# Two row maxima over the mask bytes, moved to later steps of the attention loop

## The reference

```python
scores = einsum('bsd,bmd->bsm', layernorm(x), ctx) * scale
scores = where(memory_mask[:, None, :], scores, -1e30)
readout = einsum('bsm,bmd->bsd', softmax(scores), ctx)
valid_b = any(memory_mask, axis=-1)          # one flag per sequence
x = x + where(valid_b[:, None, None], readout, 0)
```

## Time and profile before

| | before |
|---|---|
| median of 3 runs | 218.23 us (218.16 to 218.25) |
| the profiled execution, time | 218.16 us |
| the profiled execution, span in the trace | 216.4 us |
| PE busy | 209.1 us, 97% |
| DVE busy | 162.7 us, 75% |
| ACT busy | 131.1 us, 61% |
| POOL busy | 93.9 us, 43% |

### The profile page before, as it was taken

The page is one execution under the profiler, slowest core; times in us unless marked ns, Lnnn a source line. Parts: engine busy times, 40 slices in busy tenths (PEclk is TensorE's granted clock), DMA queues, the critical chain, the costliest instruction groups (busy, mean ns, idle before and its releaser), DMA issues.

```text
span 216.4 us, 4415 instructions
## 1 busy us (share of the span) xinstructions
PE 209.1 (97%) x1392; PEld 174.0 (80%) x1392; DVE 162.7 (75%) x448; ACT 131.1 (61%) x248; POOL 93.9 (43%) x83
## 2 busy tenths in 40 slices
PE   7899999998998999999999999999999999999995
PEld 2687677775686899889889899899898898898893
DVE  3789699778668658888898777686785785786754
ACT  3549898768522614766866676675765666676340
POOL 7799999305002010247535733623614615516000
PEclk9999999999999999999999999999999999999999
DMA  5995430000000000022452144043042142110002
GB/s 166 331 386 183 145 101 2 3 2 3 0 0 0 3 2 0 0 75 75 145 148 79 67 145 145 1 145 128 17 145 92 53 145 64 82 48 0 0 0 98
DMA packets 8062, 17.45 MB, mean 81 GB/s; under 512 B 960, under 2 KB 3184, under 8 KB 7920
## 3 DMA queue, kind: packets, MB, share of 16 engines
q1 hardware_dynamic: 7616, 16.97, 23.9%
q10 hardware_dynamic: 432, 0.31, 0.5%
HBM read 16.75 MB, written 0.52 MB: 80 GB/s over the span
## 4 chain that ended last, share of the span: by engine, by line
PE 76%; DVE 13%; ACT 3%; issue 3%; DMA 2%; POOL 1%; SPq 0%; DVEq 0%; ACTq 0%
PE PS L1294 35%; PE PS L1310 20%; DVE masked L819 4%; PE PS L1173 3%; PE PS L1158 3%; DMA wqkv<-wqkv_d 2%; PE PS L1146 2%; PE PS L1109 2%; PE PS L1339 2%; ACT pr L515 1%; PE PS L1261 1%; PE PS L1095 1%; DVE pt L838 1%; DVE osum L812 1%; PE PS L1167 1%
## 5 line engine op out<-in xcount | busy, mean ns | idle before, releaser
L343 POOL TENSOR_TENSOR WLg<-raw_g,WHg 128x1024 fp32r<-128x1024 f32 x16 | 38.5, 2406 | 68.3 <-ACT WHg L475 68.1
L1294 PE MATMUL PS<-XH,WHg 128*128 128x512 f32 x120 | 47.0, 391 | 0.0
L1294 PE MATMUL PS<-XL,WHg 128*128 128x512 f32 x120 | 46.9, 391 | 0.0
L1294 PE MATMUL PS<-XH,WLg 128*128 128x512 f32 x120 | 46.7, 389 | 0.0
L945 DVE TENSOR_SCALAR pt<-pt 128x512 f32<-128x512 f32 x30 | 23.7, 790 | 20.8 <-ACT pt L608 20.8
L1310 PE MATMUL PS<-WHd,HH 128*128 128x256 f32 x120 | 34.0, 283 | 0.2 <-DVE HL L954 0.2
L1310 PE MATMUL PS<-WLd,HH 128*128 128x256 f32 x120 | 34.0, 283 | 0.0
L1310 PE MATMUL PS<-WHd,HL 128*128 128x256 f32 x120 | 33.9, 283 | 0.0
L614 ACT ACTIVATE HH<-pt 128x512 fp32r<-128x512 f32 x30 | 18.9, 630 | 18.0 <-DVE pt L949 18.0
L608 ACT ACTIVATE pt<-PS,bup 128x512 f32<-128x512 f32 x30 | 20.7, 689 | 13.4 <-PE PS L1294 13.4
L515 ACT ACTIVATE pr<-masked,nmax 128x128 f32<-128x128 f32 x64 | 23.8, 448 | 7.0 <-DVE nmax L819 5.5
(11 more groups left out here) (196 smaller groups left out, 371.4 us busy)
## 6 DMA issues: line engine op xcount, KB each, us to landing
raw_g<-we_d SPq DMA_DIRECT2D x16, 512.0 KB, 4.0
raw_w<-we_d SPq DMA_DIRECT2D x16, 256.0 KB, 2.7
ctxT<-ctxT_d SPq DMA_DIRECT2D x1, 1024.0 KB, 10.3
ctx_sb<-ctx_d SPq DMA_DIRECT2D x1, 1024.0 KB, 12.3
wqkv<-wqkv_d SPq DMA_DIRECT2D x3, 256.0 KB, 4.7
out_d<-x SPq DMA_DIRECT2D x4, 128.0 KB, 1.8
rows<-rows_d SPq DMA_DIRECT2D x1, 264.0 KB, 6.2
x<-x_d ACTq DMA_DIRECT2D x2, 128.0 KB, 3.1
```

Source lines behind the costliest of these rows:

```text
L343: g.tensor_tensor(WLg[slot][:, :, :, :].rearrange("p k g f -> p (k g f)"), raw_g[slot][:, :], WHg[slot][:, :, :, :].rearrange("p k g f -> ...
L1294: i = t.matmul(PS[:, 2 * m + part, :], w[slot][:, k, part, m * P:(m + 1) * P], xx[:, k, :], start=(n == 0), stop=(n == 3 * KD - 1))
```

## The change

The two instructions of L847 leave steps 7 and 8 and stand in steps 10 and 12 (the eleventh and the thirteenth step, since v counts from 0). Nothing else changes: the same instructions, the same semaphores and the same operands on every engine.

```diff
                 if v == 5:
                     take_values(1)
-                if v in (7, 8):
-                    b = v - 7
+                if v in (10, 12):
+                    b = (v - 10) // 2
                     dve.wait_ge(mask_in, 16)
                     v_.tensor_reduce(valid[:, b:b + 1], mask8[:, b * M:(b + 1) * M], AX.X, ALU.max).then_inc(valid_done, 1)
                 if v == TAIL - 1:
```

## The result

The changed kernel takes 219.23 us (median of 6 executions, 218.92 to 219.38), the kernel before 218.24 us (6, 218.15 to 218.5): a ratio of 1.0044, 95% interval 1.0033 to 1.0054. It is slower by about 1 us. The two profiled executions, 219.26 and 218.16, are 1.10 apart, like their spans.

A forecast was written before the change was run, and what follows sets the result against it. PE's scores were taken to bound steps 8 and 10, DVE's queue the path through `att` and behind `pt` of step 12. -0.00 - 0.04 + 0.59 + 0.59 = +1.14 us on 218.16 gave 219.30 us; range 218.6 to 219.8.

The forecast's parts named there:

- What step 7 gives: DVE, step 8: PE's scores set the start of `masked`, flag or no flag; gain 0.00 us.
- What step 8 gives: DVE, steps 9 and 10: step 9 moves up 0.57 us, but PE's scores hold step 10; gain 0.04 us.
- What step 10 costs: DVE ahead of `rsum` and `att`: the flag delays PE's second turn; cost 0.59 us, 0.55 with the 0.04 taken off.
- What step 12 costs: DVE behind `pt`: idle time is over, so the flag delays the residual and steps 13 and 14; cost 0.59 us.
- POOL: POOL's `pen` multiplications, later with the flags, end near 50.4, 0.8 us before the power of step 14; costs nothing.
- The sum: Whole kernel: gains and costs of the four places add to +1.14 us, giving 219.30 us.
- The port rival: DVE's `xn` beside POOL's late `pen`: the shared port lock blocks DVE, up to 2.05 us; over 219.9, chance 0.04.
- The rival that both moves cancel: DVE bounds steps 7 to 10: removals give 1.25 us, new places cost 1.18, sum -0.07; chance 0.10.

The follow-up runs named there:

- no_flags: Against the kernel before, both flag maxima left out and POOL sets the flags to 1; 218.19 us, ratio 0.9993.
- flag0_only: Against the kernel before, only the flag of sequence 0 moves, from step 7 to step 10; 218.72 us, ratio 1.0017.
- behind_att: Against the changed kernel, the flag of step 10 stands behind `rsum` and `att` instead of ahead of them; 219.23 us.
- flag1_only: Against the kernel before, only the flag of sequence 1 moves, from step 8 to step 12; 218.65 us, ratio 1.0017.
- gaps: Against the kernel before, both flags moved to DVE's idle time of step 12, ahead of `masked` and between `masked` and `pt`; 218.12 us, ratio 0.9991.
- extra: Against the kernel before, flags stay in steps 7 and 8; two more maxima into an unread tile in steps 10 and 12; 219.28 us, ratio 1.0051.
- mid13: Against the kernel before, flag 0 stays in step 7, flag 1 moves ahead of `masked` of step 13; 219.22 us, ratio 1.0052.
- step13: Against the kernel before, flag 0 stays in step 7, flag 1 moves behind `pt` of step 13; 219.22 us, run again 218.84 us.

## Why the prediction was right

*What step 7 gives: 0.00.* Right. `masked` of step 8 kept its distance to the anchor, and the wait of 0.57 for PE took the flag's place.

*What step 8 gives: 0.04.* Right: `masked` of step 10 came 0.04 earlier, and no_flags, which gives up both old places, gained 0.04. Which of PE's waits held the 0.04 (the value products behind `osum`, as I put it, or the turns behind the exponentials) was not tested by itself. My argument for a small value, that PE has no gap there, was weaker than it looked: the turns of step 10, without an idle time in the view, took 0.97 with the flags in place, when they began ahead of the last exponentials' end, and 0.87 without. What PE gained by that ended at its wait for `att`.

*What step 10 costs: 0.59.* Right in size: `rsum` and PE's turn came 0.56 later with the 0.04 taken off, and flag0_only gave +0.61. My account of what waits was incomplete. I named the first `att`; behind_att showed that the second one sets PE's start with a slack of only 0.08, so the flag would have cost most of its time (0.50) behind the first too. And PE's idle time before the turn, which I put at about 0.8, is 0.96, for the reason just given.

*What step 12 costs: 0.59.* Right: the distance from `pt` to the residual grew from 0.48 to 1.06, flag1_only gave +0.55, and gaps showed that the same step costs nothing ahead of `pt`.

*POOL: nothing.* Right; I had its power at 51.2 and it came at 51.20, after 0.75 us of idle time. extra has `pen` early and costs the same.

*The sum, +1.14.* By the traces +1.15; by the medians 0.99. The start of the program is part of the medians and varies by more than the 0.16 between the two.

*The port rival.* Its mechanism exists: mid13 shows `xn` held until POOL's multiplication is done, and step13 shows POOL held by `xn`. In the changed kernel `pen` ends at 50.45 and `xn` starts at 51.02; the margin was 0.57 us, and I had put it at 0.65. This agrees with the exclusive lock that the Trainium skill, "SBUF — State Buffer", section "SBUF: two separate sides", describes: in both cases the one that came second is the one that took longer, by 0.35 and 0.26 us. How it looks when a VectorE instruction starts within a GpSimd one that is itself being held, as the second `xn` of step13 does, the two traces don't settle. The rival that both moves cancel failed at the condition I had given: PE's scores of step 8 did not come earlier, and those of step 10 only by 0.03.

## What to carry to other kernels

A chain of waits that names an engine proves little where two engines are equally late: compare the start of the instruction with the moment at which its other producer would have let it go. A fixed distance that appears wherever the wait is certain (0.31 us here) finds such a tie before anything is run. Filler work belongs in front of an instruction that waits, not behind it: between two places one instruction apart (gaps and flag1_only) lay 0.56 us by the traces. A row without idle time is no proof that its engine was not held: the group of turns in step 10 got shorter, 0.97 to 0.87 us, once its inputs came earlier. And before an instruction is called free, look for a second wait on the same engine, perhaps for a buffer and not for data.

## What was unexpected in the hardware

An operation of DVE from SBUF to SBUF (`xn`, 128x256 in 0.35 us) and a multiplication on POOL (128x512 in 2.01 us) hold each other up, in both directions. In mid13 an `xn` that started at 50.55 while POOL was at work took 0.698 us and ended 0.14 after POOL's end at 51.11. In step13 POOL's multiplication, started at 50.52 with one `xn` running and the next due at 50.67, took 2.267 us, and both `xn` kept their 0.35. The delay is smaller than the overlap each time: from the start of the one that was held to the end of the other lie 0.56 us in mid13, of which 0.35 were lost, and 0.49 in step13 (to 51.01, the end of the second `xn`), of which 0.26 were lost. That POOL waited for both `xn` is my estimate from these numbers. `masked`, which reads PSUM and SBUF, kept its usual length beside POOL's multiplications: 0.28 us for 128 columns in mid13 at 49.64, between POOL's start at 47.00 and its end at 51.11, and 0.28 at 46.63 in the kernel before, where POOL was idle.
